# Rows of the heavy stage's first two batches prepared in the light stage, its zero columns on ScalarE

## The chip, the cores and the metric

One core of a Trainium2 chip runs the whole program in one launch. The metric is the device time of one execution in microseconds (us); of several runs the median is given. TensorE (PE in the rows) multiplies matrices, VectorE (DVE), ScalarE (ACT) and GpSimd (POOL) work on elements, and SyncE (SP) issues the transfers. Each engine takes its own instructions in program order and waits on semaphores for the others.

## What is computed

The program chains four layers on x of 16 x 512 tokens of 128 numbers: an attention with a distance kernel, a feed-forward layer, a state-space layer, and the same feed-forward layer again. The change lies in the feed-forward layer, which stands twice in the program (f1 and f2). Cut to what matters, it is:

```python
def _L0_ffn_ref(x, ...):
    light = local_attn(_ln(x, ln_w, ln_b), Wqkv, Wout_l)   # windowed attention, all tokens
    sq, iq = route(x, rt_q, NQ)                            # 64 tokens of each batch for queries
    skv, ikv = route(x, rt_kv, NKV)                        # 128 tokens of each batch for keys and values
    xq = x[br, iq]
    xkv = x[br, ikv]
    heavy = heavy_attn(xq, xkv, skv, gamma, Wq, Wkv, Wout_h, null_kv)   # begins with rms norm of xq, xkv
    out = jnp.broadcast_to(null_q[None, None, :], (b, n, d))
    out = out.at[br, iq].set(heavy)
    return out + light
```

## The kernel before

`stage_light` computes the local attention of all 16 batches and, beside it, the routing. Its loop has 64 steps, `step(t)`, four for each batch, and each step has two units. For a unit PE writes scores, VectorE takes maxima, ScalarE the exponentials, VectorE the reciprocals, GpSimd multiplies by them (`normalise`, L1481), PE turns the result and VectorE copies it out of PSUM (`f1l_pt`, L1192 to L1195), and PE multiplies by the values. Into these steps VectorE also puts the search for the routed tokens (`pick`), whose last pieces run in steps 60 and 61 (L1236, L1239, L1241, L1243). The projections of a batch (from `xh` and `xl`, the high and the low part of its normalised rows) run one batch ahead, so those of batch 15 are through before step 60, and `z`, `xh` and `xl` are not used again in this stage.

`stage_heavy` follows behind a barrier of all engines: each engine branches into the next block when all have left the last one. It treats the batches in eight pairs. For a pair, PE first gathers the routed tokens (`gather`, L1628 and L1629): for each batch `h` of the pair it multiplies the rows of the batch by a one-hot matrix `g`, eight matmuls of 128x256, alternating between the low part `yl` and the high part `yh` of the rows. `g` has 192 columns of one-hots, which VectorE writes for each batch (`onehots`, L1852 and L1855), and 64 columns of zeros behind them, written once for each of the two buffers at the start of the stage (L1905, VectorE). GpSimd makes `yh` and `yl` (`scaled`): it multiplies the layer's rows `y` by the rms factors `rc` into `yb` (L1814), copies this to `yh` (L1818), which rounds it, and subtracts to get `yl` (L1820). Two pairs of buffers, one for each batch of a pair, serve all batches in turn.

At the start of the stage PE first multiplies the null values by weights (`null_rows`, L1616), and then waits in `gather(0)` for `s_y` (GpSimd) and `s_g` (VectorE). When both gathers of a pair are done ScalarE takes the result out of PSUM (`tokens`, L1743, tile `gx`), and PE goes on with `queries` (L1638), `keys` (L1645), `contents` (L1653) and `scores` (L1668); nothing of a pair can start before `gx` is written. Then comes the gather of the next pair. GpSimd's program begins with `scaled(0)` and `scaled(1)`, then `scaled(2)` and `scaled(3)`, then `normalise(0, 0)` of the first pair.

Of the kernel before, what the change touches and what calls it, by code (L numbers as in the profile page):

```python
# [7 lines left out]
F32 = mybir.dt.float32  # L8
BF16 = mybir.dt.bfloat16
F32R = mybir.dt.float32r  # L10
ALU = mybir.AluOpType
# [3 lines left out]
P = 128  # L15
B, S, E = 16, 512, 128
NT = S // P
# [669 lines left out]
def stage_light(nc, K, tag, C=None):  # L687
# [13 lines left out]
    with ExitStack() as ctx:  # L701
# [3 lines left out]
        PW = P + W  # L705
        z = sb("z", [P, NT, P])
        xt = sb("xt", [P, S])
        xh = sb("xh", [P, 2, S], F32R)
        xl = sb("xl", [P, 2, S], F32R)
        qt = sb("qt", [P, 2, HP, S])  # L710
        kt = sb("kt", [P, 2, HP, S])
        vv = sb("vv", [P, 2, NT, 2, 2, 2, DH])
# [21 lines left out]
        s_xp = sem("xp")  # L734
        s_xe = sem("xe")
        s_xs = sem("xs")
        s_pp = sem("pp")
        s_pe = sem("pe")
        s_vs = [sem("vs0"), sem("vs1")]
# [719 lines left out]
        def _(pool):  # L1459
# [6 lines left out]
            def split(b):  # L1466
# [4 lines left out]
                pool.wait_ge(s_xs, 2 * b + 1)  # L1471
                nc.gpsimd.tensor_tensor(xl[:, par, :], xt[:], xh[:, par, :], ALU.subtract).then_inc(s_xs, 1)

            def normalise(n):
                u = n % UNITS
                pool.wait_ge(s_rs, n + 1)
                wait(pool, s_t, n - 1)
                r = rs[:, u % 2, :].unsqueeze(2)
                for cols, at in ((slice(0, P), 0), (slice(P, PW), HU * P)):
                    w = cols.stop - cols.start  # L1480
                    ins = nc.gpsimd.tensor_tensor(pn[:, u % 2, at:at + HU * w].rearrange("p (k c) -> p k c", k=HU),  # L1481
                                                  p[:, u % 2, :, cols], r.broadcast_to([P, HU, w]), ALU.mult)
                ins.then_inc(s_nm, 1)
# [19 lines left out]
            for t in range(T):  # L1503
                if t + 1 < T:
                    normalise(2 * t + 2)
                    normalise(2 * t + 3)
                if t % NT == TURN_AT and t // NT + 2 < B:
                    split(t // NT + 2)
                if t % NT == 1 and t // NT + 2 < B:
                    scaled(t // NT + 2)  # L1510

        work.close()
        sem.end()
# [2 lines left out]
def stage_heavy(nc, K, tag, stats, out=None):  # L1516
# [6 lines left out]
    with ExitStack() as ctx:  # L1523
# [4 lines left out]
        K1 = NKV + 1  # L1528
        GW = 256
        yb = sb("yb", [P, NT, P])  # L1530
        yh = sb("yh", [P, 2, NT, P], F32R)
        yl = sb("yl", [P, 2, NT, P], F32R)
        g = sb("g", [P, 2, NT, GW], F32R)
        gx = sb("gx", [P, 2, GC])
        rows = sb("rows", [P, M, S])
# [20 lines left out]
        s_yb = sem("yb")  # L1556
        s_nx = sem("nx")
        s_g = sem("g")
        p_w = sem("pw")
        v_w = sem("vw")  # L1560
        p_g = sem("pg")
# [50 lines left out]
        def _(pe):  # L1612
# [7 lines left out]
            def gather(m):  # L1620
                wait(pe, a_x, m)
                wait(pe, v_p, m - 1)
                for h in range(2):
                    pe.wait_ge(s_y, 2 * m + h + 1)
                    pe.wait_ge(s_g, 2 * m + h + 1)
                    at = W_[:, GB, h * GW:(h + 1) * GW]
                    for j in range(NT):
                        nc.tensor.matmul(at, yl[:, h, j, :], g[:, h, j, :], start=(j == 0), stop=False)  # L1628
                        mm = nc.tensor.matmul(at, yh[:, h, j, :], g[:, h, j, :], start=False, stop=(j == NT - 1))  # L1629
                    mm.then_inc(p_g, 1)  # L1630
# [108 lines left out]
        def _(act):  # L1739
# [43 lines left out]
            def values(m):  # L1783
# [2 lines left out]
                nc.scalar.activation(ot[:].rearrange("p c h q -> p h c q"),  # L1786
                                     W_[:, QB, :].rearrange("p (h c q) -> p h c q", h=2, c=HP), ACT.Copy).then_inc(a_ot, 1)

            for n in range(M + 1):
                if n >= 1:  # L1790
                    exps(n - 1, 0, (0, 1, 2, 3))
                    exps(n - 1, 1, (0, 1))
                if n < M:
                    tokens(n)
                if n >= 1:
                    exps(n - 1, 1, (2, 3))
                if n < M:
                    queries(n)
                    keys(n)
                if n >= 1:  # L1800
                    turned(n - 1)
                if n < M:
                    contents(n)
                if n >= 1:
                    values(n - 1)
# [4 lines left out]
        def _(pool):  # L1810
            def scaled(b):
# [1 line left out]
                t = slice(NT * b, NT * (b + 1))  # L1813
                nc.gpsimd.tensor_tensor(yb[:], K["y"][:, t, :], K["rc"][:, t].unsqueeze(2).broadcast_to([P, NT, P]),  # L1814
                                        ALU.mult).then_inc(s_yb, 1)
                pool.wait_ge(s_yb, 2 * b + 1)
                wait(pool, p_g, b - 1)
                nc.gpsimd.tensor_copy(yh[:, h], yb[:]).then_inc(s_yb, 1)  # L1818
                pool.wait_ge(s_yb, 2 * b + 2)
                nc.gpsimd.tensor_tensor(yl[:, h], yb[:], yh[:, h], ALU.subtract).then_inc(s_y, 1)  # L1820
                pool.wait_ge(s_y, b + 1)

            def normalise(m, h):
                pool.wait_ge(v_r, 2 * m + h + 1)
# [5 lines left out]
                nc.gpsimd.tensor_tensor(xp, xp, K["null_q"][:].unsqueeze(1).broadcast_to([P, 2 * NT, P]),  # L1830
                                        ALU.add).then_inc(s_nx, 1)

            scaled(0)
            scaled(1)
            for n in range(M + 1):
                if n >= 1:
                    normalise(n - 1, 0)
# [10 lines left out]
        def _(dve):  # L1848
# [52 lines left out]
                    ins = nc.vector.bn_aggr(K["mv"][:, 2 * NT * m + j, :], st6[:, j, :])  # L1901
                ins.then_inc(v_s, 1)

            for e in range(2):
                nc.vector.tensor_scalar(g[:, e, :, GC:], K["ident"][:, 0:GW - GC].unsqueeze(1)  # L1905
                                        .broadcast_to([P, NT, GW - GC]), 0.0, None, ALU.mult)
            onehots(0)
            onehots(1)
            dve.wait_ge(p_w, 1)
# [356 lines left out]
def program(nc, A, out):  # L2266
    with ExitStack() as ctx:
# [50 lines left out]
            C[n] = sb("c_" + n, [P, P])  # L2318
        for n in ("cc", "ss", "tmp", "dec"):
            C[n] = sb("c_" + n, [P, S])  # L2320
        with nc.sbuf_tensor("f1_y", [P, T, E], F32) as K["y"]:
            stage_light(nc, K, "f1", C)
            stage_heavy(nc, K, "f1", True)
        with nc.sbuf_tensor("f2_y", [P, T, E], F32) as K["y"]:
            stage_ssm(nc, K, C)
            stage_light(nc, K, "f2")
            stage_heavy(nc, K, "f2", False, out)
# [68 lines left out]
```

## Time and profile before

| | us |
|---|---|
| median of 3 runs | 1873.87 (1870.62 to 1874.62) |
| the profiled execution, its own time | 1877.24 |
| its span, from the first to the last instruction | 1875.2 |
| light stage f1, last instruction of VectorE ends | 1004.4 |
| heavy stage f1, first instruction of PE | 1004.72 |
| heavy stage f1, ScalarE begins to take out the first gather | 1013.99 |
| heavy stage f2, first instruction of PE | 1749.12 |

The rows below are read from the profiled execution. In a row of the order of time, the first number is the start of the instruction (or of a run of like instructions) in us from the start of the span, the second how long it took, then come the engine, the line, the operation, the tile written and those read, the shapes and the count; in brackets stands how long the engine had been idle before it, and what released it. "PEclk" in a table of stretches is the clock granted to TensorE as a share of 2.4 GHz; 0.50 is 1.2 GHz.

### The profile page before, as it was taken

Reading aid. Unit: us, or ns where it says so; the run is one execution under the profiler, and the core shown is the slowest. Engines: PE = TensorE matmul, PEld = TensorE weight load, DVE = VectorE, ACT = ScalarE, POOL = GpSimd, SP = SyncE. Lnnn points to the kernel's source line nnn. Section 1 sums busy time; section 2 is a strip of 40 time slices with the busy share of each in tenths; the row PEclk is TensorE's granted clock in tenths of the full one; section 3 lists DMA queues with packets and bytes.
Section 4 is the critical chain, followed back from the end, with each engine's and each line's share of the span. In section 5 each row is a group of like instructions: output and inputs, shape, how many; then the busy total and the mean of one; then the engine's idle time right before and its main releaser. Section 6 shows DMA issues by size and latency. Waiting matters only on the chain. (4 is left out here: it accounts for less than half of the span.)

```text
span 1875.2 us, 67956 instructions
## 1 busy us (share of the span) xinstructions
PE 1694.7 (90%) x27513; PEld 1302.1 (69%) x27513; DVE 1457.4 (78%) x3472; ACT 1434.4 (76%) x4088; POOL 752.5 (40%) x842
## 2 busy tenths in 40 slices
PE   3888888986999999999997996989999999998797
PEld 1444444444688888888885874668888888887586
DVE  8999999998577677877896766757777777789574
ACT  4999999995688888888773656668888888876364
POOL 2000000000254445454545866435454545454594
PEclk7999999998999999999998998989999999999898
DMA  6655655550000000101012000001010101010111
GB/s 194 153 142 143 160 136 144 125 149 4 12 20 19 20 20 15 24 14 25 14 25 47 2 2 1 1 12 23 16 25 15 25 14 26 14 25 15 45 46 46
DMA packets 80039, 91.94 MB, mean 49 GB/s; under 512 B 11696, under 2 KB 67984, under 8 KB 79728
## 3 DMA queue, kind: packets, MB, share of 16 engines
q1 hardware_dynamic: 78432, 87.15, 19.0%
q8 instruction: 220, 3.60, 0.8%
q14 instruction: 91, 0.75, 0.1%
q10 hardware_dynamic: 1296, 0.44, 0.1%
HBM read 39.68 MB, written 31.10 MB: 38 GB/s over the span
## 5 line engine op out<-in xcount | busy, mean ns | idle before, releaser
L1481 POOL TENSOR_TENSOR f1l_pn<-f1l_p,f1l_rs 128x512 f32<-128x512 f32 (+1 forms) x256 | 207.8, 833 | 264.6 <-DVE f1l_rs L1185 263.5
L1481 POOL TENSOR_TENSOR f2l_pn<-f2l_p,f2l_rs 128x512 f32<-128x512 f32 (+1 forms) x256 | 207.8, 833 | 256.0 <-DVE f2l_rs L1185 255.9
L1065 ACT ACTIVATE f2l_p<-f2l_sm,f2l_nb 128x192 f32<-128x192 f32 x512 | 214.6, 444 | 44.5 <-DVE f2l_nb L1178 44.5
L1065 ACT ACTIVATE f1l_p<-f1l_sm,f1l_nb 128x192 f32<-128x192 f32 x512 | 214.4, 443 | 42.4 <-DVE f1l_nb L1178 42.4
L412 PE MATMUL r_acc<-r_pr,r_vp 128*32 128x128 f32 (+2 forms) x3584 | 191.8, 330 | 7.1 <-DVE r_pr L625 6.0
L522 ACT ACTIVATE r_pr<-r_far 128x1536 f32<-128x1536 f32 x128 | 194.2, 1517 | 3.3 <-PE r_far L396 3.0
L617 DVE SCALAR_TENSOR_TENSOR r_pr<-r_pr,k_lo,r_cap 128x512 f32<-128x512 f32 x256 | 179.4, 741 | 6.5 <-ACT r_pr L522 6.3
L625 DVE TENSOR_SCALAR r_pr<-r_pr,k_hi,k_lo 128x768 f32<-128x768 f32 x256 | 164.3, 682 | 0.0
L522 ACT ACTIVATE r_pr<-r_near 128x1024 f32<-128x1024 f32 x128 | 138.5, 1082 | 1.1 <-PE r_near L383 1.1
L1486 POOL MEMSET k_rtz<- 128x608 f32 x1 | 0.6, 605 | 332.2 <-POOLq L683 332.2
L1178 DVE TENSOR_REDUCE f2l_nb<-f2l_sm 128x4 f32<-128x768 f32 x128 | 116.0, 947 | 8.2 <-PE f2l_sm L885 8.2
L1178 DVE TENSOR_REDUCE f1l_nb<-f1l_sm 128x4 f32<-128x768 f32 x128 | 115.9, 947 | 6.2 <-PE f1l_sm L885 6.2
L412 PEld LDWEIGHTS r_acc<-r_pr,r_vp 128*32 128x32 f32 x3584 | 87.2, 110 | 47.4 <-issue 29.0
L1065 ACT ACTIVATION_READ_ACCUMULATOR f2l_p<-f2l_sm,f2l_nb 128x1 f32 x512 | 117.2, 229 | 0.0
L1065 ACT ACTIVATION_READ_ACCUMULATOR f1l_p<-f1l_sm,f1l_nb 128x1 f32 x512 | 116.8, 228 | 0.0
L885 PE MATMUL f2l_sm<-f2l_kt,f2l_qt 64*64 64x128 f32 (+1 forms) x3584 | 99.4, 248 | 0.4 <-ACT f2l_p L1065 0.4
L885 PE MATMUL f1l_sm<-f1l_kt,f1l_qt 64*64 64x128 f32 (+1 forms) x3584 | 99.0, 248 | 0.0
L1203 DVE TENSOR_TENSOR f1l_ot<-f1l_xa,f1l_late 128x256 f32<-128x256 f32 x128 | 53.5, 418 | 57.6 <-ACT f1l_late L1057 57.0
L1203 DVE TENSOR_TENSOR f2l_ot<-f2l_xa,f2l_late 128x256 f32<-128x256 f32 x128 | 53.5, 418 | 57.4 <-ACT f2l_late L1057 56.8
L885 PEld LDWEIGHTS f2l_sm<-f2l_kt,f2l_qt 64*64 64x64 f32 x3584 | 92.9, 134 | 0.9 <-ACT f2l_p L1065 0.6
L925 PE MATMUL f2l_xa<-f2l_pt,f2l_vv 64*64 64x128 f32 x2048 | 85.8, 276 | 8.2 <-DVE f2l_pt L1193 3.4
L885 PEld LDWEIGHTS f1l_sm<-f1l_kt,f1l_qt 64*64 64x64 f32 x3584 | 92.8, 134 | 0.2 <-issue 0.2
(497 smaller groups left out, 5203.8 us busy)
## 6 DMA issues: line engine op xcount, KB each, us to landing
rbf_rows<-r_part SPq DMA_DIRECT2D x112, 128.0 KB, 2.3
r_qs<-rbf_rows SPq DMA_DIRECT2D x60, 192.0 KB
r_ks<-rbf_rows SPq DMA_DIRECT2D x60, 192.0 KB
f1l_vs<-f1l_vv SPq DMA_DIRECT2D x64, 128.0 KB, 2.4
f2l_vs<-f2l_vv SPq DMA_DIRECT2D x64, 128.0 KB, 2.4
rbf_rows<-r_part SPq DMA_DIRECT2D x16, 384.0 KB, 3.2
rbf_rows<-r_part SPq DMA_DIRECT2D x16, 256.0 KB, 3.2
out<-k_x SPq DMA_DIRECT2D x8, 512.0 KB, 3.2
```

Source lines behind the costliest of these rows:

```text
L412: mm = nc.tensor.matmul(acc[32 * g:32 * g + 32, q0:q0 + n], vp[:, par, t, g, 32 * q:32 * q + 32], pr[:, (PAIRS * b + 2 * q + g // 2) % RIN ...
L522: nc.scalar.activation(pr[:, n % RING, :, cols], src, ACT.Exp).then_inc(done, 1)
L617: nc.vector.scalar_tensor_tensor(on, on, K["lo"][:, h:h + 1], cap[:, h, :].unsqueeze(1).broadcast_to([P, NT, P]), ALU.max, ALU.min)
L625: ins = nc.vector.tensor_scalar(off, off, hi, lo, ALU.min, ALU.max)
L885: mm = nc.tensor.matmul(sm[64 * w:64 * w + 64, u % 2, e, cc * PW + P * side:cc * PW + P * side + kn], qt[r, par, c, at:at + W], kt[r, par, ...
L925: nc.tensor.matmul(xa[64 * e:64 * e + 64, r, cc * P:(cc + 1) * P], vv[rows, par, i, cc, g, e, :], pt[rows, u % 2, k * P:(k + 1) * P], star ...
L1065: ins = nc.scalar.activation(p[:, u % 2, k, :], sm[:, u % 2, k // 2, k % 2 * PW:(k % 2 + 1) * PW], ACT.Exp, bias=nb[:, u % 2, k:k + 1], ac ...
L1178: nc.vector.tensor_reduce(nb[:, u % 2, :], sm[:, u % 2, :, 0:2 * PW].rearrange("p a (k c) -> p a k c", k=2), AX, ALU.max, negate=True).the ...
L1203: nc.vector.tensor_tensor(ot[:, u // 2 % 2, 2 * g:2 * g + 2, :], xa[:, 0, 0:2 * P].rearrange("p (c q) -> p c q", q=P), late[:, u % 2, :].r ...
L1481: ins = nc.gpsimd.tensor_tensor(pn[:, u % 2, at:at + HU * w].rearrange("p (k c) -> p k c", k=HU), p[:, u % 2, :, cols], r.broadcast_to([P, ...
L1486: nc.gpsimd.memset(K["rtz"][:], 0.0).then_inc(s_rt, 1)
```

## The change

The buffers of the high and low rows, `xh` and `xl`, now outlive the light stage: they are allocated around both stages, the light stage uses them as before, and the heavy stage uses the same memory under its names `yh` and `yl`. At the end of steps 60 to 63 of the light stage GpSimd has a new function, `tokens(b, part)`, that does for batches 0 and 1 what `scaled(0)` and `scaled(1)` did in the heavy stage, with `z` in the place of `yb`: step 60 multiplies and copies batch 0, step 61 subtracts it, step 62 multiplies and copies batch 1, step 63 subtracts it. The heavy stage's GpSimd program begins with `scaled(2)`, and `gather(0)` waits no longer for rows. The zero columns of `g` are written by ScalarE as its first two instructions of the heavy stage, by a copy of `ident` with scale 0; `gather(0)` waits for them by a semaphore of its own (`a_g`).

```diff
@@ stage_light
-        xh = sb("xh", [P, 2, S], F32R)
-        xl = sb("xl", [P, 2, S], F32R)
+        xh, xl = K["xh"], K["xl"]
@@ stage_light, gpsimd
+            def tokens(b, part):
+                whole = z[:].rearrange("p j d -> p (j d)")
+                if part == 0:
+                    if b == 0:
+                        pool.wait_ge(s_xp, B)
+                        pool.wait_ge(s_pp, USES * B)
+                    t = bass.ds(b * NT, NT)
+                    nc.gpsimd.tensor_tensor(z[:], K["y"][:, t, :],
+                                            K["rc"][:, t].unsqueeze(2).broadcast_to([P, NT, P]), ALU.mult).then_inc(s_h, 1)
+                    pool.wait_ge(s_h, 3 * b + 1)
+                    nc.gpsimd.tensor_copy(xh[:, b, :], whole).then_inc(s_h, 1)
+                else:
+                    pool.wait_ge(s_h, 3 * b + 2)
+                    nc.gpsimd.tensor_tensor(xl[:, b, :], whole, xh[:, b, :], ALU.subtract).then_inc(s_h, 1)
+                    pool.wait_ge(s_h, 3 * b + 3)
...
                 if t % NT == 1 and t // NT + 2 < B:
                     scaled(t // NT + 2)
+                if t // NT == B - 1:
+                    tokens(t % NT // 2, t % NT % 2)
@@ stage_heavy
-        yh = sb("yh", [P, 2, NT, P], F32R)
-        yl = sb("yl", [P, 2, NT, P], F32R)
+        yh, yl = (K[n].rearrange("p h (j d) -> p h j d", j=NT) for n in ("xh", "xl"))
@@ stage_heavy, tensor, gather
-                    pe.wait_ge(s_y, 2 * m + h + 1)
+                    wait(pe, s_y, 2 * m + h - 1)
                     pe.wait_ge(s_g, 2 * m + h + 1)
+                    if m == 0:
+                        pe.wait_ge(a_g, h + 1)
@@ stage_heavy, scalar
+            for e in range(2):
+                nc.scalar.activation(g[:, e, :, GC:], K["ident"][:, 0:GW - GC].unsqueeze(1)
+                                     .broadcast_to([P, NT, GW - GC]), ACT.Copy, scale=0.0).then_inc(a_g, 1)
@@ stage_heavy, gpsimd (the waits on s_yb and s_y in scaled count from batch 2)
-            scaled(0)
-            scaled(1)
@@ stage_heavy, vector
-            for e in range(2):
-                nc.vector.tensor_scalar(g[:, e, :, GC:], K["ident"][:, 0:GW - GC].unsqueeze(1)
-                                        .broadcast_to([P, NT, GW - GC]), 0.0, None, ALU.mult)
```

The order of the instructions shows what has moved, here for f1; f2 reads alike. In the changed kernel the lines stand some 16 to 23 further down (L1497 is `normalise`, L1481 to L1487 are `tokens`, L1837 to L1843 are `scaled`). First GpSimd at the end of the light stage and the start of the heavy stage, before:

```order
L1481 TENSOR_TENSOR f1l_pn<-f1l_p,f1l_rs 128x256
L1512 UNCONDITIONAL_BRANCH
L1809 UNCONDITIONAL_BRANCH [waits barrier_Pool_Activation_PE_DVE_SP_gather]
L1814 TENSOR_TENSOR f1h_yb<-f_y,k_rc 128x512
L1818 CAST f1h_yh<-f1h_yb 128x512 [waits h_yb]
L1820 TENSOR_TENSOR f1h_yl<-f1h_yb,f1h_yh 128x512 [waits h_yb]
L1814 TENSOR_TENSOR f1h_yb<-f_y,k_rc 128x512 [waits h_y]
```

and now:

```order
L1497 TENSOR_TENSOR f1l_pn<-f1l_p,f1l_rs 128x256
L1481 TENSOR_TENSOR f1l_z<-f_y,k_rc 128x512
L1484 CAST f_xh<-f1l_z 128x512 [waits l_h]
L1487 TENSOR_TENSOR f_xl<-f1l_z,f_xh 128x512 [waits l_h]
L1530 UNCONDITIONAL_BRANCH [waits l_h]
L1832 UNCONDITIONAL_BRANCH [waits barrier_Pool_Activation_PE_DVE_SP_gather]
L1837 TENSOR_TENSOR f1h_yb<-f_y,k_rc 128x512
L1841 CAST f_xh<-f1h_yb 128x512 [waits h_pg,h_yb]
L1843 TENSOR_TENSOR f_xl<-f1h_yb,f_xh 128x512 [waits h_yb]
```

Batch 1 is now prepared behind the last normalisation of the light stage, ahead of the branch, and the first copy of the heavy stage is that of batch 2, which waits for PE's first gather (`h_pg`); batch 0 stands in the same way behind the normalisations of steps 60 and 61.

VectorE at the start of the heavy stage, before:

```order
L1209 TENSOR_TENSOR k_x<-k_x,f1l_xa 128x128 [waits l_w]
L1512 UNCONDITIONAL_BRANCH
L1847 UNCONDITIONAL_BRANCH [waits barrier_Pool_Activation_PE_DVE_SP_release]
L1905 TENSOR_SCALAR f1h_g<-k_ident 128x4x64 x2
L1852 TENSOR_TENSOR f1h_g<-k_iota,k_place 128x4x64
L1855 TENSOR_TENSOR f1h_g<-k_iota,k_place 128x4x128
```

and now:

```order
L1209 TENSOR_TENSOR k_x<-k_x,f1l_xa 128x128 [waits l_w]
L1530 UNCONDITIONAL_BRANCH
L1868 UNCONDITIONAL_BRANCH [waits barrier_Pool_Activation_PE_DVE_SP_release]
L1873 TENSOR_TENSOR f1h_g<-k_iota,k_place 128x4x64
L1876 TENSOR_TENSOR f1h_g<-k_iota,k_place 128x4x128
```

The one-hots of batch 0 are now the first instructions of VectorE in the stage; the two zero-column instructions stand on ScalarE ahead of the instruction that takes out the gather:

```order
L1170 ACTIVATE k_place<-f1l_pj 128x128 [waits l_tt]
L1530 UNCONDITIONAL_BRANCH
L1758 UNCONDITIONAL_BRANCH [waits barrier_Pool_Activation_PE_DVE_SP_release]
L1810 ACTIVATE f1h_g<-k_ident 128x4x64 x2
L1763 ACTIVATE f1h_gx<-f1h_ps,k_gam_h 128x384 [waits h_pg]
L1769 ACTIVATE f1h_qt<-f1h_ps 128x512 [waits h_pq]
```

These two instructions wait for nothing; before, the take-out (`f1h_gx`) was ScalarE's first instruction of the stage.

## Rows read from the trace of the kernel before

**Rows 1.** The page's busy time, share of the span and instructions of each engine.

```profile
PE 1694.7 (90%) x27513; PEld 1302.1 (69%) x27513; DVE 1457.4 (78%) x3472; ACT 1434.4 (76%) x4088; POOL 752.5 (40%) x842
```

**Rows 2.** Order of time, PE, start of the heavy stage f1, columns as told above.

```profile
1004.72 1.86 PE L1616 MATMUL f1h_ps<-k_wout_h,k_null_v 128*4 128x128 f32 x8 [0.65 <-PEq L1512]
1008.66 0.55 PE L1628 MATMUL f1h_ps<-f1h_g,f1h_yl 128*128 128x256 f32 x1 [2.07 <-DVE f1h_g L1855]
...
1010.29 0.41 PE L1629 MATMUL f1h_ps<-f1h_g,f1h_yh 128*128 128x256 f32 x1
1011.88 0.58 PE L1628 MATMUL f1h_ps<-f1h_g,f1h_yl 128*128 128x256 f32 x1 [1.18 <-POOL f1h_yl L1820]
...
1014.63 2.08 PE L1638 MATMUL f1h_ps<-f1h_gx,k_wq_h 128*128 128x128 f32 x8 [0.67 <-ACT f1h_gx L1743]
1016.50 3.02 PE L1645 MATMUL f1h_ps<-f1h_gx,k_wk_h 128*128 128x256 f32 x8
```

**Rows 3.** Order of time, PE, start of the heavy stage f2.

```profile
1749.12 1.86 PE L1616 MATMUL f2h_ps<-k_wout_h,k_null_v 128*4 128x128 f32 x8 [0.65 <-PEq L1512]
...
1756.28 0.58 PE L1628 MATMUL f2h_ps<-f2h_g,f2h_yl 128*128 128x256 f32 x1 [1.18 <-POOL f2h_yl L1820]
```

**Rows 4.** Order of time, DVE, start of the heavy stage f1.

```profile
1004.73 1.37 DVE L1905 TENSOR_SCALAR f1h_g<-k_ident 128x256 fp32r<-128x256 f32 x2 [0.33 <-PEq L1512]
1006.02 0.82 DVE L1852 TENSOR_TENSOR f1h_g<-k_iota,k_place 128x256 fp32r<-128x256 f32 x1
1006.77 1.75 DVE L1855 TENSOR_TENSOR f1h_g<-k_iota,k_place 128x512 fp32r<-128x512 f32 x1
```

**Rows 5.** Order of time, POOL, end of the light stage f1, start of the heavy stage.

```profile
990.93 3.33 POOL L1481 TENSOR_TENSOR f1l_pn<-f1l_p,f1l_rs 128x512 f32<-128x512 f32 x4 [3.27 <-DVE f1l_rs L1185]
1004.71 1.04 POOL L1814 TENSOR_TENSOR f1h_yb<-f_y,k_rc 128x512 f32<-128x512 f32 x1 [10.44 <-POOLq L1512]
1005.81 0.75 POOL L1818 CAST f1h_yh<-f1h_yb 128x512 fp32r<-128x512 f32 x1
1006.64 1.32 POOL L1820 TENSOR_TENSOR f1h_yl<-f1h_yb,f1h_yh 128x512 fp32r<-128x512 f32 x1
...
1010.24 1.59 POOL L1820 TENSOR_TENSOR f1h_yl<-f1h_yb,f1h_yh 128x512 fp32r<-128x512 f32 x1
```

**Rows 6.** Order of time, ACT, end of the light stage f1, start of the heavy stage.

```profile
1001.10 0.38 ACT L1057 ACTIVATE f1l_late<-f1l_xa 128x256 f32<-128x256 f32 x1 [1.36 <-PE f1l_xa L936]
...
1013.99 0.58 ACT L1743 ACTIVATE f1h_gx<-f1h_ps,k_gam_h 128x384 f32<-128x384 f32 x1 [12.28 <-PE f1h_ps L1629]
```

**Rows 7.** Stretches: length, busy us of PE, PEld, DVE, ACT, POOL; PEclk, DMA, GB/s.

```profile
1018.00:1019.00 1.00, 1.00 (x4) 0.79 (x4) 0.00 (x0) 0.55 (x1) 1.00 (x1) 0.62 0.00 0
1019.00:1020.00 1.00, 1.00 (x5) 0.68 (x4) 0.00 (x0) 0.50 (x2) 0.04 (x1) 1.00 0.00 0
```

**Rows 8.** Order of time, PE, the second pair's gather, queries and keys in f1.

```profile
1022.20 0.38 PE L1628 MATMUL f1h_ps<-f1h_g,f1h_yl 128*128 128x256 f32 x1
...
1024.09 0.28 PE L1629 MATMUL f1h_ps<-f1h_g,f1h_yh 128*128 128x256 f32 x1
1025.36 1.16 PE L1638 MATMUL f1h_ps<-f1h_gx,k_wq_h 128*128 128x128 f32 x8 [0.99 <-ACT f1h_gx L1743]
1026.36 1.89 PE L1645 MATMUL f1h_ps<-f1h_gx,k_wk_h 128*128 128x256 f32 x8
```

**Rows 9.** Order of time, POOL, steps 60 and 61 of the light stage f1.

```profile
976.10 3.92 POOL L1481 TENSOR_TENSOR f1l_pn<-f1l_p,f1l_rs 128x512 f32<-128x512 f32 x4 [3.33 <-DVE f1l_rs L1185]
983.22 2.06 POOL L1481 TENSOR_TENSOR f1l_pn<-f1l_p,f1l_rs 128x512 f32<-128x512 f32 x2 [3.20 <-DVE f1l_rs L1185]
```

**Rows 10.** Order of time, DVE, the same steps.

```profile
980.94 1.20 DVE L1239 TENSOR_TENSOR_SCAN f1l_some<-f1l_one,f1l_picks 32x512 f32<-32x512 f32 x1
```

**Rows 11.** Order of time, PE, the same steps.

```profile
985.28 0.67 PE L925 MATMUL f1l_xa<-f1l_pt,f1l_vv 64*64 64x128 f32 x16 [1.56 <-DVE f1l_pt L1193]
```

**Rows 12.** One line's instructions in f1: duration ns min/median/max, first and last start.

```profile
L1193 DVE COPY f1l_pt<-f1l_xa x128: 393/414/425, 503.0 to 998.0; 128x256 f32<-128x256 f32 x128
```

More of the change, by code:

```diff
@@ L736, in stage_light @@
         s_xs = sem("xs")
+        s_h = sem("h")
         s_pp = sem("pp")
@@ L1558, in stage_heavy @@
         s_g = sem("g")
+        a_g = sem("ag")
         p_w = sem("pw")
@@ L1815, in scaled @@
                                         ALU.mult).then_inc(s_yb, 1)
-                pool.wait_ge(s_yb, 2 * b + 1)
+                pool.wait_ge(s_yb, 2 * b - 3)
                 wait(pool, p_g, b - 1)
                 nc.gpsimd.tensor_copy(yh[:, h], yb[:]).then_inc(s_yb, 1)
-                pool.wait_ge(s_yb, 2 * b + 2)
+                pool.wait_ge(s_yb, 2 * b - 2)
                 nc.gpsimd.tensor_tensor(yl[:, h], yb[:], yh[:, h], ALU.subtract).then_inc(s_y, 1)
-                pool.wait_ge(s_y, b + 1)
+                pool.wait_ge(s_y, b - 1)
             def normalise(m, h):
@@ L2320, in program @@
             C[n] = sb("c_" + n, [P, S])
-        with nc.sbuf_tensor("f1_y", [P, T, E], F32) as K["y"]:
+        with (nc.sbuf_tensor("f1_y", [P, T, E], F32) as K["y"], nc.sbuf_tensor("f1_xh", [P, 2, S], F32R) as K["xh"],
+              nc.sbuf_tensor("f1_xl", [P, 2, S], F32R) as K["xl"]):
             stage_light(nc, K, "f1", C)
             stage_heavy(nc, K, "f1", True)
-        with nc.sbuf_tensor("f2_y", [P, T, E], F32) as K["y"]:
+        with (nc.sbuf_tensor("f2_y", [P, T, E], F32) as K["y"], nc.sbuf_tensor("f2_xh", [P, 2, S], F32R) as K["xh"],
+              nc.sbuf_tensor("f2_xl", [P, 2, S], F32R) as K["xl"]):
             stage_ssm(nc, K, C)
```

## The prediction

> **What bounds the kernel now.** I read the page's busy shares first, then the order of time on PE around both places where the light stage hands over to the heavy stage, then that of the other engines in the same microseconds, then the granted clock, and last the steps of the light stage into which the moved work is put.
>
> PE is busy for 90% of the span and GpSimd for 40% [rows 1], so a move of work off GpSimd matters only where PE waits for GpSimd. At the head of the heavy stage it does. PE ends `null_rows` at 1004.72 + 1.86 = 1006.58 and starts the first gather at 1008.66; the wait is put down to the one-hots [rows 2]. The second gather starts at 1011.88, after a wait for the low rows of batch 1, and ScalarE takes the result out at 1013.99 [rows 2, 6]. GpSimd ends the low rows of batch 0 at 1006.64 + 1.32 = 1007.96 and those of batch 1 at 1010.24 + 1.59 = 1011.83 [rows 5]. VectorE spends 1.37 on zero columns and ends the first one-hots at 1006.77 + 1.75 = 1008.52 [rows 4]. So the first gather waits for VectorE, with GpSimd 0.56 behind the same wait, and the second waits for GpSimd alone. Until the take-out nothing else of the pair can run: ScalarE had been idle for 12.28 [rows 6]. From the block's first matmul to the take-out are 13.99 - 4.72 = 9.27. In f2 the second gather also starts 7.16 after the first matmul, 1756.28 against 1749.12 [rows 3], so what f1 gains f2 gains too.
>
> All this runs at the low level of the clock. The stretch in which the granted clock goes up is 1018 to 1019 (0.62, then 1.00) [rows 7]: 1.2 GHz before it, 2.4 GHz behind it. What PE did before that was to work without a break from 1014.63; before, its work was cut by the two waits and by the take-out [rows 2].
>
> **The head of the heavy stage: 3.2 us each.** With the rows ready, the first gather waits for `null_rows` (1006.58), the zero columns and the first one-hots. The zero columns go to ScalarE: a row of 128x256 there took 0.38, one of 128x384 took 0.58 [rows 6]; two of them from 1004.72 on end between 1005.5 and 1005.9, under `null_rows`. If that cover were gone they would cost at most the 1.2 themselves. The one-hots: a VectorE instruction of this kind stands still while GpSimd works. The one at 1006.77 ran until 0.56 after GpSimd's subtraction ended (1008.52 against 1007.96) [rows 4, 5]; I take 0.56 as its own duration, and no more than that for the smaller one ahead of it. GpSimd still starts with a multiplication (1.04, until 1005.75 [rows 5]), then stands in its wait for the first gather. So the first one-hots end by 1005.75 + 0.56 + 0.56 = 1006.87, and 0.14 later, as at 1008.52 and 1008.66 [rows 2, 4], PE can start: 1007.0 at the latest of this reckoning, 1006.6 at the earliest (`null_rows`). I take 1006.9. The first gather lasts 1.85 (1008.66 to 1010.29, and 0.22 for the last of the eight), the second 2.11 up to the take-out (1011.88 to 1013.99) [rows 2, 6]; the second one-hots, 1.12 after the first, are in time. Take-out: 1006.9 + 1.85 + 2.11 = 1010.86 instead of 1013.99, a gain of 3.1 to 3.4; I take 3.2. The lower bound takes the one-hots as slow as they are now: 1008.52 - 1006.02 = 2.5 [rows 4] from 1004.73, so PE starts at 1007.37, and the second one-hots, 2.5 later still, hold up the second gather by 0.65 more; that leaves 2.0. VectorE's 1.37 of zero columns is part of this gain, not another term.
>
> What is late next is the hop through ScalarE (0.64 from 1013.99 to 1014.63 [rows 2, 6]) and PE's own work. GpSimd's copy of batch 2 now waits for the first gather at about 1008.8; behind it in its queue stand batches 2 and 3 and the normalisation of the first pair. With 0.75, 1.32, 1.04, 0.75 and 1.32 [rows 5] it is through by about 1014.5, and PE wants these rows behind the scores, at 1022.20 now [rows 8], some 3 to 6 earlier then. That is hidden by at least 1.5. SP's transfers stand in the same place as before.
>
> **The clock: 2.3 us each.** Without the two waits PE works from 1004.72 to 1010.4 with one gap of about 0.3. That is longer than its work from 1014.63 to the rise at 1018.6. So I expect the rise during the gathers, some 10 us earlier, and price it by rows at either level: queries 2.08 against 1.16, keys 3.02 against 1.89 [rows 2, 8], together 2.05; a gather 1.85 against 8 x (1024.09 - 1022.20) / 15 = 1.0 [rows 2, 8], so up to 0.85 more if the rise comes ahead of the second gather. From 2.0 to 2.9; I take 2.3. If the rise comes only behind the take-out, this term is near 0. The Trainium skill, TensorE: Matmul & The Clock Gate (Part 1: The HAM clock gate), says that the place of this rise shifts between runs of one kernel; no run here shows that yet.
>
> **The light stage: 0.2 us lost each.** `tokens` issues six GpSimd instructions per stage, 2 x (1.04 + 0.75 + 1.32) = 6.2 by [rows 5]. Batch 0's multiplication and copy fall behind the normalisations that end at 980.02, and the next normalisation starts at 983.22 after 3.20 of idle time [rows 9]; 1.79 fit, also with a wait in between. The subtraction (1.32) falls into the 3.27 ahead of 990.93, and batch 1 (3.1) into the 10.44 behind 994.26 [rows 5]. So no normalisation is late. What can be late is VectorE: its scan starts at 980.94 [rows 10], while GpSimd's multiplication would run until about 981.1, and reads SBUF alone as the one-hots do. PE waits for VectorE just behind it (1.56 at 985.28 [rows 11]), so this wait is on the path: 0.2. Bounds: 0, if the scan doesn't mind, and 1.0, if it also waits for the copy (981.1 + 0.1 + 0.75). Nothing is taken out of the light stage, so it can't gain. VectorE's copies out of PSUM don't mind GpSimd: L1193 took 393 to 425 ns in all 128 cases [rows 12], many of them beside a normalisation.
>
> The Trainium skill, SBUF — State Buffer (SBUF: two separate sides), says that VectorE and GpSimd share a port pair as an exclusive lock for a whole instruction, taken on VectorE's side by operations with two SBUF inputs. By that rule the scan loses the 0.2, and without it 0; the end at 1008.52, 0.56 behind GpSimd's, agrees with it.
>
> **Sum.** 3.2 + 2.3 - 0.2 = 5.3 per stage, 10.6 for both. The profiled execution's own 1877.24 would become 1866.6. It lies 3.4 above the median of the runs shown, 1873.87; taken from the median, the forecast is 1863.3.
>
> **The rivals.**
> - *The clock rises early in one stage only, or in neither.* For it: the take-out still cuts PE's work, and before, two pieces of some 2 us each and a third of 1.9 behind a gap of 0.67 had not raised it by 1018 [rows 2, 7]. Against it: the first stretch is now 5.7 long. One stage only: 1863.3 + 2.3 = 1865.6; neither: 1867.9.
> - *Another wait takes the place of GpSimd's*, so that the change doesn't do what it says: one-hots as slow as now (a gain of 2.0), the scan at its worst (1.0), no earlier clock. 2 x 1.0 gained, 1871.9, within 0.2%. For it: VectorE was the last releaser of the first gather [rows 2]. Against it: its slowness came from GpSimd's work beside it, of which 1.04 is left.
> - *GpSimd's moved work stops VectorE in the light stage.* The mechanism is the lock between the two, in steps 60 to 63: if VectorE stood still for the whole of `tokens`, the light stage would lose 6.2 per stage against 3.2 gained, without the earlier clock. 1873.87 + 2 x 3.0 = 1879.9. It decides from a loss of 3.2 per stage on. For it: PE waits for VectorE there [rows 11]. Against it: VectorE's work there is mostly out of PSUM, in which GpSimd's work doesn't show [rows 12], and half of the 6.2 falls where VectorE itself waits for the last outputs.
>
> **How the numbers follow.** Forecast, early clock in both stages: 0.40. In one: 0.23; in neither: 0.21; another wait: 0.10; the light stage loses more: 0.06. The range takes in the first three with their bounds: at the low end 3.4 + 2.9 - 0 = 6.3 per stage, 1861.3, and a little less for the spread of the runs (3.3 below the median): 1860.0; at the high end no early clock, 2.0 - 0.2 = 1.8 per stage, 1870.3, so 1870.5. A measurement of this kernel can tell about 0.2%, 3.7 us, from no change. Faster by more: 0.40 + 0.23 + 0.21 = 0.84; within: 0.10; slower: 0.06.
>
> **What would show it.** In the changed kernel's order of time: the first gather within 0.5 of the end of `null_rows`, the second right behind it, and the take-out 5.5 to 6.2 after the block's first matmul, where it is 9.27 now. The clock at 1.00 before the queries, which then take about 1.2, not 2.1. The scan's end at most 0.3 later against the normalisation ahead of it, and the last 28 us of the light stage (976.10 to 1004.4) as long as before within 0.5. Wrong would be: a first gather that still waits for VectorE beyond 1.0, queries at 2.08, or VectorE instructions in steps 60 to 63 that take longer than now beside `tokens`.

## The result, and the profile after

The changed kernel takes 1857.79 us (median of 4 runs, 1855.63 to 1863.65) against 1872.71 of the kernel before beside it: a ratio of 0.992, 95% interval 0.9902 to 0.9939. It is faster, as forecast, but by 14.9 us (by the interval 11.4 to 18.4) instead of 10.6, and the time lies 2.2 below the low end of the range. The profiled execution took 1859.21, its span 1857.4 (before: 1877.24 and 1875.2). Two of all the executions here, one of the kernel before (2116.78) and one of the changed kernel (1952.04), were in a slower state of the chip and are left out of every median below.

Order of time, PE, end of the light stage f1 and head of the heavy stage, changed kernel (it answers to [rows 2]):

```profile
1003.74 1.16 PE L947 MATMUL f1l_xa<-k_wout_l,f1l_ot 128*128 128x128 f32 x8 [0.60 <-DVE f1l_ot L1203]
1005.55 1.03 PE L1634 MATMUL f1h_ps<-k_wout_h,k_null_v 128*4 128x128 f32 x8 [0.65 <-PEq L1530]
1007.51 0.39 PE L1648 MATMUL f1h_ps<-f1h_g,f_xl 128*128 128x256 f32 x1 [0.93 <-DVE f1h_g L1876]
...
1009.41 0.28 PE L1649 MATMUL f1h_ps<-f1h_g,f_xh 128*128 128x256 f32 x1
1010.36 1.16 PE L1658 MATMUL f1h_ps<-f1h_gx,k_wq_h 128*128 128x128 f32 x8 [0.67 <-ACT f1h_gx L1763]
...
1014.90 1.11 PE L1688 MATMUL f1h_ps<-f1h_kt,f1h_qt 64*64 64x129 f32 x32
```

The wait for GpSimd's low rows (1.18 in [rows 2]) is gone: the sixteen matmuls of both gathers run in a row from 1007.51. The queries start 4.8 behind the block's first matmul, where it was 9.9, and take 1.16 instead of 2.08. `null_rows` takes 1.03 instead of 1.86, and the light stage's last output ahead of it 1.16: here PE comes into the heavy stage at 2.4 GHz already. In f2 of the same execution it does not:

```profile
1736.08 2.08 PE L947 MATMUL f2l_xa<-k_wout_l,f2l_ot 128*128 128x128 f32 x8 [0.60 <-DVE f2l_ot L1203]
1738.80 1.86 PE L1634 MATMUL f2h_ps<-k_wout_h,k_null_v 128*4 128x128 f32 x8 [0.65 <-PEq L1530]
1740.76 0.58 PE L1648 MATMUL f2h_ps<-f2h_g,f_xl 128*128 128x256 f32 x1
...
1742.00 0.40 PE L1649 MATMUL f2h_ps<-f2h_g,f_xh 128*128 128x256 f32 x1
1742.21 0.31 PE L1648 MATMUL f2h_ps<-f2h_g,f_xl 128*128 128x256 f32 x1
...
1744.26 0.94 PE L1658 MATMUL f2h_ps<-f2h_gx,k_wq_h 128*128 128x128 f32 x6 [0.67 <-ACT f2h_gx L1763]
```

Here the first gather starts without a wait, and its matmuls change from 0.40 to 0.28 towards its end. The stretches of the changed kernel show the clock (columns as in [rows 7]; the granted clock stands behind POOL's busy time):

```profile
1006.00:1008.00 2.00, 1.07 (x10) 0.74 (x8) 2.00 (x4) 0.25 (x1) 0.58 (x1) 1.00 0.39 137
...
1740.00:1742.00 2.00, 1.90 (x10) 1.37 (x8) 2.00 (x7) 0.00 (x0) 0.00 (x0) 0.50 0.80 232
1742.00:1744.00 2.00, 1.59 (x12) 1.38 (x11) 1.45 (x4) 0.38 (x1) 1.14 (x2) 0.94 1.04 227
```

So in f1 it is 1.00 from the start, and in f2 it rises at about 1742.2, 3.4 behind the block's first matmul, where it was some 14 ([rows 7], within 1018 to 1019, against 1004.72).

VectorE and ScalarE at the head of f1, order of time, changed kernel ([rows 4, 6]):

```profile
1005.55 1.30 DVE L1873 TENSOR_TENSOR f1h_g<-k_iota,k_place 128x256 fp32r<-128x256 f32 x1 [0.32 <-PEq L1530]
1006.78 0.68 DVE L1876 TENSOR_TENSOR f1h_g<-k_iota,k_place 128x512 fp32r<-128x512 f32 x1
```

```profile
1005.53 0.72 ACT L1810 ACTIVATE f1h_g<-k_ident 128x256 fp32r<-128x256 f32 x2 [2.08 <-PEq L1530]
1009.73 0.58 ACT L1763 ACTIVATE f1h_gx<-f1h_ps,k_gam_h 128x384 f32<-128x384 f32 x1 [3.48 <-PE f1h_ps L1649]
```

ScalarE's zero columns are through at 1006.25, in `null_rows`' shadow. The take-out comes 4.18 behind the block's first matmul (9.27 before).

GpSimd in the last steps of the light stage f1 and at the head, and VectorE's scan, order of time, changed kernel ([rows 5, 9, 10]):

```profile
981.73 1.04 POOL L1481 TENSOR_TENSOR f1l_z<-f_y,k_rc 128x512 f32<-128x512 f32 x1
982.83 1.47 POOL L1484 CAST f_xh<-f1l_z 128x512 fp32r<-128x512 f32 x1
984.96 2.06 POOL L1497 TENSOR_TENSOR f1l_pn<-f1l_p,f1l_rs 128x512 f32<-128x512 f32 x2 [0.67 <-DVE f1l_rs L1185]
...
997.08 0.61 POOL L1484 CAST f_xh<-f1l_z 128x512 fp32r<-128x512 f32 x1
...
1005.54 1.04 POOL L1837 TENSOR_TENSOR f1h_yb<-f_y,k_rc 128x512 f32<-128x512 f32 x1 [6.50 <-POOLq L1530]
```

```profile
982.68 1.20 DVE L1239 TENSOR_TENSOR_SCAN f1l_some<-f1l_one,f1l_picks 32x512 f32<-32x512 f32 x1
```

The scan takes 1.20 as before. It is GpSimd's copy that waits, 1.47 where the second one takes 0.61, and the normalisation behind it still has 0.67 to spare.

**Where the 17.8 between the two spans went**, by the starts of the same instructions on PE. The first scores of f1 before, in the order of time:

```profile
1021.16 1.11 PE L1668 MATMUL f1h_ps<-f1h_kt,f1h_qt 64*64 64x129 f32 x32
```

From the heavy stage's first matmul in f1 to the first of the state-space stage: 122.4 before, 114.4 after, a gain of 8.0, of which 7.1 lie ahead of the first scores (16.44 against 9.35 behind the block's first matmul). In f2, from the same matmul to the end: 126.1 and 118.6, a gain of 7.5, of which 6.3 ahead of the first scores (16.29 against 9.99). The state-space stage, from its first matmul to the end of its last: 101.1 and 99.6, a gain of 1.5. The rest, 0.8, lies in all that comes ahead and in the light stage of f2; what comes ahead alone differs by up to 7 between executions of one kernel (the heavy stage of f1 starts between 1003.67 and 1010.60 in four profiles of the changed kernel). The profile of before is of an execution 4.5 above the median beside the result, that of the changed kernel of one 1.4 above its own, which is why 17.8 here is 14.9 in the medians.

### The profile page after: what moved, and what is told of

Its sections match the earlier page's. It is cut to its first block and busy times, and to the rows that moved or that the text cites. A ratio compares the mean times of both kernels' runs of the same rounds, so it can differ in the third digit from the quotient of the medians.

```text
span 1857.4 us, 67964 instructions
## 1 busy us (share of the span) xinstructions
PE 1684.3 (91%) x27513; PEld 1292.5 (70%) x27513; DVE 1448.5 (78%) x3468; ACT 1436.0 (77%) x4092; POOL 753.7 (41%) x842
## 5 line engine op out<-in xcount | busy, mean ns | idle before, releaser
L1497 POOL TENSOR_TENSOR f1l_pn<-f1l_p,f1l_rs 128x512 f32<-128x512 f32 (+1 forms) x256 | 207.9, 834 | 259.6 <-DVE f1l_rs L1185 258.6
L1497 POOL TENSOR_TENSOR f2l_pn<-f2l_p,f2l_rs 128x512 f32<-128x512 f32 (+1 forms) x256 | 207.9, 834 | 250.7 <-DVE f2l_rs L1185 250.7
```

## The experiments

The theory: both head waits fell, and the clock with them, so the gain lies ahead of the first scores; the light stage loses little. The rivals: the zero columns did it; the moved GpSimd work has a price in the light stage; or the clock alone did it. All of the first group ran beside each other and one set of runs of before (1873.26).

**The changed kernel again.**

> The changed kernel as it is, run again on another occasion, for its time over more runs and a second profile. Theory A (the rows' waits at both heads of the heavy stage are gone and TensorE's clock is up early there; what exceeds this differs from run to run with the places at which the clock happens to fall): the heads give 6.3 to 7.1 us each, so 13 to 15 us below the kernel before, and from block start to the first scores 9.3 to 10.0 us in both stages where the kernel before took 16.3 to 16.4; whether the light stage's last output runs at 1.2 or 2.4 GHz may come out either way in each stage. Theory B (the light stage itself became shorter by the change, 27.4 us instead of 28.3 us for its last part in f1): the last output runs at 2.4 GHz again in f1.

1857.11, ratio 0.9922 (0.9906 to 0.9939). Its heads were the other way round: f1 came in at 1.2 GHz (first scores after 10.1) and f2 at 2.4 (9.3). Over four profiles of the changed kernel five of eight heads came in at 2.4 GHz (9.33 to 9.35) and three at 1.2 (9.99 to 10.09); the mean is 9.6. So which one does is not fixed by the program. A head that comes in at 2.4 GHz also ends its light stage 0.9 sooner (22.87 against 23.78 from VectorE's scan to the heavy stage, f1 and f2 of the first profile). Over the kernels here that put no dummy matmuls into the light stage, nine of fourteen heads behind a light stage with the moved work came in at 2.4 GHz, and one of six behind one without it; whether the moved work makes this likelier is not shown by so few.

**The rows moved, the zero columns left on VectorE.**

```diff
@@ changed kernel, stage_heavy: a_g and its waits out
-            for e in range(2):
-                nc.scalar.activation(g[:, e, :, GC:], ... ACT.Copy, scale=0.0).then_inc(a_g, 1)
@@ vector
+            for e in range(2):
+                nc.vector.tensor_scalar(g[:, e, :, GC:], ... 0.0, None, ALU.mult)
             onehots(0)
```

> Only the rows are moved; the zero columns stay on VectorE ahead of the one-hots. Theory A: VectorE's first instruction stands still for GpSimd's 1.04 us, the first one-hots come 0.6 to 0.7 us later than in the changed kernel, at about 2.5 us after the block's start, and the time is 0.5 to 2.5 us above the changed kernel's, so 11 to 14 us below the kernel before. Theory C (the zero columns on VectorE were the larger part of the wait): 4 us or more above the changed kernel's.

1860.09, ratio 0.9932 (0.9919 to 0.9945). PE and VectorE at its head, order of time:

```profile
1002.20 1.03 PE L1633 MATMUL f1h_ps<-k_wout_h,k_null_v 128*4 128x128 f32 x8 [0.65 <-PEq L1530]
1004.56 0.39 PE L1645 MATMUL f1h_ps<-f1h_g,f_xl 128*128 128x256 f32 x1 [1.33 <-DVE f1h_g L1870]
```

```profile
1002.20 1.37 DVE L1920 TENSOR_SCALAR f1h_g<-k_ident 128x256 fp32r<-128x256 f32 x2 [0.33 <-PEq L1530]
1003.50 0.41 DVE L1867 TENSOR_TENSOR f1h_g<-k_iota,k_place 128x256 fp32r<-128x256 f32 x1
1003.83 0.68 DVE L1870 TENSOR_TENSOR f1h_g<-k_iota,k_place 128x512 fp32r<-128x512 f32 x1
```

The two zero-column instructions of f1 apart (duration ns min/median/max, first and last start):

```profile
L1920 DVE TENSOR_SCALAR f1h_g<-k_ident x2: 280/726/1172, 1002.2 to 1003.3; 128x256 fp32r<-128x256 f32 x2
```

The first gather starts 2.36 behind the block's first matmul, 0.4 later than in the changed kernel. The first zero-column instruction takes 1.17 beside GpSimd's multiplication (1002.18 to 1003.22), the second, behind it, 0.28, and the one-hots 0.41 and 0.68. In the changed kernel the first one-hots take 1.30 instead, because now they meet that multiplication. What VectorE loses at the head is thus the multiplication, whichever of its instructions stands first: most of what ScalarE takes off VectorE is lost again, and the rows carry nearly the whole gain. Both heads came in at 2.4 GHz, with the first scores after 9.73 and 9.74.

**The zero columns on ScalarE, the rows left.** The same instructions the other way, in the kernel before.

> Only the zero columns go to ScalarE; the rows are prepared in the heavy stage as before. Theory A: the second gather still waits for the low rows of batch 1, about 7.1 us after the block's start, so the time is that of the kernel before within 1.5 us. Theory C: 4 us or more below the kernel before.

1875.30, ratio 1.0013 (1.0003 to 1.0024): nothing gained. The first gather started 3.5 instead of 3.9 behind the block's first matmul, the second where it was, since it waits for GpSimd, and the first scores came at 16.3 and 16.4. Of the two parts it is the zero columns that are worth nothing alone.

**The light stage's work twice.** `tokens` as in the changed kernel, added to the kernel before; its result is not used.

> The kernel before, with the six GpSimd instructions of the preparation added to the light stage's last four steps (their result is not used; the heavy stage prepares its rows as before). It prices what the moved work costs the light stage. Theory A: nothing, the time of the kernel before within 1.5 us, and the scan still takes 1.20 us. The prediction's step: 0.2 us per stage, at most 1.0 per stage. Theory B: the light stage gets shorter by it, 1.8 us or more in all below the kernel before.

1873.64, ratio 0.9996 (0.9982 to 1.001). No cost of the moved work in the light stage can be told: the interval is from 3.4 us faster to 1.9 slower, and from VectorE's scan (1.20) to the heavy stage it is 22.85 in f1 and 23.77 in f2, where two light stages without that work have 22.86 and 23.78 at the same clock. f1 of the profiled execution came into the heavy stage at 2.4 GHz, with the old waits. Order of time, PE, and the stretches:

```profile
1006.84 1.03 PE L1635 MATMUL f1h_ps<-k_wout_h,k_null_v 128*4 128x128 f32 x8 [0.65 <-PEq L1531]
1010.78 0.55 PE L1647 MATMUL f1h_ps<-f1h_g,f1h_yl 128*128 128x256 f32 x1 [2.90 <-DVE f1h_g L1874]
...
1014.00 0.58 PE L1647 MATMUL f1h_ps<-f1h_g,f1h_yl 128*128 128x256 f32 x1 [1.17 <-POOL f1h_yl L1839]
...
1016.74 2.08 PE L1657 MATMUL f1h_ps<-f1h_gx,k_wq_h 128*128 128x128 f32 x8 [0.67 <-ACT f1h_gx L1762]
```

```profile
1010.00:1011.00 1.00, 0.22 (x1) 0.25 (x2) 1.00 (x2) 0.00 (x0) 0.92 (x2) 0.77 1.05 217
1011.00:1012.00 1.00, 1.00 (x6) 1.00 (x7) 1.00 (x2) 0.00 (x0) 0.94 (x2) 0.50 1.05 207
...
1020.00:1021.00 1.00, 1.00 (x5) 0.80 (x4) 0.00 (x0) 0.44 (x1) 1.00 (x1) 0.61 0.00 0
```

The clock was up at 1006.84, fell in the wait of 2.90, and rose again only in 1020 to 1021. The first scores came after 16.4, as in the kernel before. So with the waits left empty this head, which came in at 2.4 GHz, lost the clock; in the changed kernel's five it stayed up to the queries.

**The clock without the rows.** A second group, beside 1873.6 of before. In the kernel before, dummy matmuls stand in PE's two waits, so that the clock rises while the gathers still wait; their result is not used.

```diff
@@ kernel before, stage_heavy, tensor
+            def busy(k):
+                for c in range(k):
+                    nc.tensor.matmul(W_[:, TB, 0:P], K["wq_h"][:, 0:P], K["wq_h"][:, 0:P], start=True, stop=True)
...
                 for h in range(2):
+                    if m == 0:
+                        busy((4, 2)[h])
                     pe.wait_ge(s_y, 2 * m + h + 1)
```

> The kernel before with nothing moved, but PE kept at work in the two waits at the head of the heavy stage: four 128x128 fp32 matmuls, not used, behind null_rows and two between the gathers. It prices the clock by itself, with the waits for the rows left in. Theory A (clock and waits both count): the clock is up 4 to 7 us after the block's start, queries take about 1.2 us instead of 2.1 us, and the first scores start at 12.7 to 13.5 us after the block's start instead of 16.2 to 16.5: 6 to 7 us below the kernel before. Theory D (only the waits count, the clock comes back where it did): the time of the kernel before within 1.5 us.

1868.17, ratio 0.9974 (0.9964 to 0.9984), 5.4 us, a little less than expected. Order of time, PE, f1:

```profile
1008.28 1.86 PE L1616 MATMUL f1h_ps<-k_wout_h,k_null_v 128*4 128x128 f32 x8 [0.65 <-PEq L1512]
1010.08 1.90 PE L1622 MATMUL f1h_ps<-k_wq_h 128*128 128x128 f32 x8
1012.23 0.36 PE L1634 MATMUL f1h_ps<-f1h_g,f1h_yl 128*128 128x256 f32 x1 [0.25 <-DVE f1h_g L1861]
...
1015.45 0.39 PE L1634 MATMUL f1h_ps<-f1h_g,f1h_yl 128*128 128x256 f32 x1 [1.59 <-POOL f1h_yl L1826]
...
1017.34 1.16 PE L1644 MATMUL f1h_ps<-f1h_gx,k_wq_h 128*128 128x128 f32 x8 [0.67 <-ACT f1h_gx L1749]
...
1021.88 1.11 PE L1674 MATMUL f1h_ps<-f1h_kt,f1h_qt 64*64 64x129 f32 x32
```

Both gathers still start where they did, the second 7.17 behind the block's first matmul as in [rows 2], and the first scores come at 13.6 instead of 16.4, in f2 as well: this is the clock alone, 2.8 per stage. The changed kernel with the same `null_rows` (1.86) has them at 10.0 to 10.1: the waits are worth 3.6 more. The clock alone is thus less than half of the gain, and that rival falls.

**GpSimd's first multiplication later.** It waits until VectorE has written both one-hots.

```diff
@@ changed kernel, stage_heavy, gpsimd, scaled
+                if b == 2:
+                    pool.wait_ge(s_g, 2)
                 nc.gpsimd.tensor_tensor(yb[:], K["y"][:, t, :], ...
```

> The changed kernel, with GpSimd's first multiplication of the heavy stage made to wait for the one-hots of batches 0 and 1, so that VectorE has its first instructions for itself. Theory A (what is left of the first gather's wait is VectorE standing still for GpSimd's 1.04 us): the first one-hots need 0.41 + 0.68 us, the first gather starts at 1.1 to 1.3 us after the block's start where the clock is up at the block's start (1.9 now) and at 1.9 to 2.0 where it isn't (null_rows ends then), 0.2 to 1.7 us below the changed kernel in all. Rival: GpSimd becomes late with batches 2 and 3, and the second pair's gather waits for it: at or above the changed kernel.

1857.41, ratio 0.9916 (0.9900 to 0.9932), beside 1858.26 of the changed kernel (third time, below): not told apart. VectorE and PE at the head of f2, order of time:

```profile
1739.43 0.42 DVE L1875 TENSOR_TENSOR f2h_g<-k_iota,k_place 128x256 fp32r<-128x256 f32 x1 [0.33 <-PEq L1530]
```

```profile
1739.43 1.03 PE L1634 MATMUL f2h_ps<-k_wout_h,k_null_v 128*4 128x128 f32 x8 [0.65 <-PEq L1530]
1740.51 0.38 PE L1648 MATMUL f2h_ps<-f2h_g,f_xl 128*128 128x256 f32 x1
```

The one-hots take 0.42 where they took 1.30, and the wait of 0.93 ahead of the first gather is gone: it starts 1.1 behind the block's first matmul instead of 1.9, and the first scores come at 8.5. In a head that comes in at 1.2 GHz `null_rows` (1.86) covers nearly the whole of it (9.8, against 10.0 without).

**The clock kept up into the heavy stage.** As the last, with twelve dummy matmuls in PE's last waits of the light stage (two and three in each of steps 62 and 63, two ahead of the last output; the first expectation below counts eleven).

```diff
@@ stage_light, tensor
+            def busy(k):
+                for c in range(k):
+                    nc.tensor.matmul(sm[:, 0, 0, 0:P], K["ident"][:], K["ident"][:], start=True, stop=True)
...
+                if t + 2 >= T:
+                    pe.wait_ge(s_ex, UNITS * B - 1)
+                    busy(2)
```

> As e5_mult_later, and PE is kept at work in its waits of the light stage's last two steps by seven... eleven unused 128x128 fp32 matmuls in all (two ahead of the first and three ahead of the second values of steps 62 and 63, two ahead of the last output), so that the clock stays up into the heavy stage. Theory A: the last output takes 1.1 to 1.2 us and null_rows 1.03 us in both stages, the first scores start 8.4 to 8.7 us after the block's start in both, 2 to 4 us below the changed kernel in all. Rival: the added matmuls stand in the way of the values and the outputs, and the light stage's last part gets longer by as much or more: at or above the changed kernel.

1857.40 (0.9914, 0.9897 to 0.9931), and a second time, in a third group (before: 1871.79) and beside 1857.36 of the changed kernel, 1857.99 (0.9929, 0.9909 to 0.9948):

> The changed kernel with the two additions of the last call: GpSimd's first multiplication of the heavy stage waits for the one-hots of batch 1, and twelve dummy matmuls of 128x128 stand in TensorE's last waits of the light stage. Theory that the clock at the head is the whole rest of the gain: both heads have block start to scores 8.4 instead of 9.3 to 10.1, so 2 to 3 us below the changed kernel beside it. Rival, that the dummies stand in the way of real work at the light stage's end or that the runs of the changed kernel have the high clock there about as often: equal to the changed kernel within 1.5 us.

All four heads came in at 2.4 GHz, with the first scores at 8.45 to 8.46, 1.1 less than the changed kernel's mean. In the time nothing can be told from the changed kernel, and the 2 to 4 us expected did not show; 2.3 us for both heads was to be seen at best, and the clock fell elsewhere: in the second profile it stood low for 3.4 from 984 on, in the last steps of f1's light stage, and the stretch from the scan to the end of that stage was 1.4 longer (24.26 against 22.87). f2 of the run with the later multiplication, without dummy matmuls, has such a stretch too (24.38).

**The changed kernel a third and a fourth time**, as the neighbours of these:

> The changed kernel beside the three above on the same chip, for a direct comparison and a third profile: 1855 to 1860 us; block start to first scores 9.3 us where the clock is up at the block's start and 10.0 us where it isn't.

> The changed kernel again, as the neighbour of the next two runs. All theories: 1857 to 1859 us, ratio to before 0.992.

1858.26 and 1857.36, ratios 0.9923 (0.9910 to 0.9936) and 0.9929 (0.9908 to 0.9949).

**The same at the head of the state-space stage.** As the kernel with the light stage's twelve dummy matmuls, and nine more behind that stage's first transpose, where PE waits for the input.

```diff
@@ stage_ssm, tensor
+            for k in range(9):
+                nc.tensor.matmul(tp[:, 0, 0:P], K["ident"][:], K["ident"][:], start=True, stop=True)
```

> As the run before it, with nine more dummy matmuls of 128x128 on TensorE at the start of the state-space stage, behind its first transpose, where TensorE waits for the input transfer. Theory that the clock at a stage's head is worth its rows at either level wherever a stage begins: the first products of that stage (3.7 us at the low level in the changed kernel, 1.9 at the high one) end some 1.8 earlier, so 1 to 2 us below the run before it, 1854 to 1856. Rival, that VectorE's scan and not TensorE sets the time there: equal to the run before it within 1 us.

1855.48, ratio 0.9918 (0.9901 to 0.9935). Order of time, PE, the changed kernel first, then this one:

```profile
1119.94 0.45 PE L2211 MATMUL s_xx<-k_ident,k_c_bb 128*128 128x128 f32 x1 [3.94 <-PEq L1955]
...
1128.11 3.49 PE L2230 MATMUL s_xx<-s_ut,s_bbt 128*64 128x512 f32 x8 [1.30 <-ACT s_ut L2150]
...
1133.82 1.94 PE L2230 MATMUL s_xx<-s_ut,s_bbt 128*64 128x512 f32 x8 [1.21 <-ACT s_ut L2150]
```

```profile
1119.34 0.45 PE L2223 MATMUL s_xx<-k_ident,k_c_bb 128*128 128x128 f32 x1 [3.94 <-PEq L1967]
1119.58 3.38 PE L2225 MATMUL s_tp<-k_ident 128*128 128x128 f32 x18
...
1126.87 1.94 PE L2244 MATMUL s_xx<-s_ut,s_bbt 128*64 128x512 f32 x8 [1.54 <-ACT s_ut L2162]
...
1131.03 1.94 PE L2244 MATMUL s_xx<-s_ut,s_bbt 128*64 128x512 f32 x8 [1.20 <-ACT s_ut L2162]
```

The second block of products starts 11.7 instead of 13.9 behind the transpose: 2.2 gained at that place. The median is 1.9 to 2.5 below its two neighbours, and the lowest of all kernels here, but the runs of the three overlap (1854.79 to 1858.32 against 1854.35 to 1859.93 with the light stage's dummies alone and 1854.37 to 1862.23 of the changed kernel), so that it beats the changed kernel is likely and not shown.

## Why the prediction was too small

The mechanism was right and sizes were off: the clock's term was priced for one level of the clock only, and the state-space stage, in which 1.5 came, was put at nothing without a reason.

**Right.** What bounds the head (two waits, then the take-out), that both stages gain, the sign, and that the clock adds to it. The queries take 1.16 in all eight heads.

**Wrong: the sizes in the sum, 5.3 per stage.** The gain ahead of the first scores is 16.4 - 9.6 = 6.8 on average:

- *The head, forecast 3.2:* 3.6, from 13.6 with the clock alone to 10.0 with the rows ready. The sum took both gathers at their length at the low clock, which puts the second 4.0 behind the block's first matmul. The clock rises during the first gather: in f2 the second starts after 3.7 (sixteen matmuls in a row from 1740.76), and the take-out comes after 4.2 to 4.9 instead of the forecast 5.5 to 6.2. The gain by the waits and the gain by the clock are not two independent terms, and no run has the rows ready and the clock low throughout, so the waits by themselves are not measured.
- *The clock, forecast 2.3, at most 2.9:* 2.8 if PE comes in at 1.2 GHz, and 0.7 more (10.0 against 9.3) if it comes in at 2.4, which five of eight heads did; 3.2 on average. This is the step of the sum that failed: the bound of 2.9 was too low. It allowed for a rise ahead of the second gather at the earliest, and did not ask what a head without waits does with a clock that is already up: it keeps it. The rows of before had shown both heads at 1.2 GHz (`null_rows` 1.86, [rows 2, 3]) and I took that for fixed.
- *The light stage, forecast -0.2:* 0 as far as can be told. VectorE's scan was expected to stand behind GpSimd's multiplication. It started 0.09 before that ended and took 1.20; GpSimd's copy waited for it instead, in 0.67 and more of idle time. The Trainium skill, SBUF — State Buffer (SBUF: two separate sides), says that the one that starts first has the shared ports for its whole instruction. By that rule the loss depends on who is first, and the trace agrees in the main: the copy took 1.47 behind the scan's start, the one-hots 1.30 beside GpSimd's multiplication and 0.42 without it; but the copy ended only 0.42 behind the scan, less than the 0.61 it takes alone, and the scan, begun in the last 0.09 of the multiplication, took no longer for it.

Two readings of the rows were wrong as well. The 1.37 of zero columns is mostly a stop beside GpSimd's multiplication, 1.17 and 0.28 in one stage; it passes to whichever VectorE instruction comes first, so moving them is worth 0.4 per head at the scores (9.73 against 9.35). And the larger one-hots take 0.68 alone, not 0.56.

Both stages together: 2 x 6.8 = 13.6 against the 10.6 of the sum.

**Not in the sum at all: 1.5 in the state-space stage.** That stage lasts 100.9 to 101.1 in the profiles of before and of the experiments with only part of the change or with dummy matmuls in the kernel before, and 99.6 to 99.7 in all four of the changed kernel. Order of time, PE, and a stretch of before; then PE of the changed kernel:

```profile
1164.48 2.86 PE L2223 MATMUL s_yy<-k_c_g,s_v 64*128 64x128 f32 x32
1167.28 2.84 PE L2228 MATMUL s_yy<-k_c_dd,s_ut 128*128 128x128 f32 x16
```

```profile
1166.00:1168.00 2.00, 2.00 (x17) 1.78 (x14) 0.69 (x2) 2.00 (x6) 1.36 (x2) 0.50 0.00 0
```

```profile
1157.45 2.06 PE L2241 MATMUL s_yy<-k_c_g,s_v 64*128 64x128 f32 x32
1159.44 2.05 PE L2246 MATMUL s_yy<-k_c_dd,s_ut 128*128 128x128 f32 x16
```

Before, the clock falls once more there and these take 2.86 and 2.84; in the changed kernel it does not. The waits around it are the same in both (2.03 and 2.47 or 2.48 ahead of `s_ty`). What makes the fall come or stay out is not settled; no run here varied it alone. 13.6 + 1.5 = 15.1, near the 14.9 measured. The run with the rows alone fits: its heads gain 2 x 6.6, its state-space stage next to nothing, and it came out 13.2 below the kernel before.

**The range.** Its low end stood on 6.3 per stage, 12.6 (1861.3, less 1.3 for the spread). The heads gave 1.0 more than that, the state-space stage 1.5, and the kernel before was 1.2 lower beside the result (1872.71) than where the forecast set out (1873.87). With the heads alone and from 1873.87 the time would have been 1860.3, just inside: that it fell outside is in part chance.

The rivals: that the clock rises early in one stage or in none fell, since it was up ahead of the queries in all eight heads of the changed kernel. Another wait did take a place, VectorE's first one-hots (0.93 at 1007.51), as feared; it is too short to matter, and where PE comes in at 1.2 GHz it is covered. That the moved work stops VectorE in the light stage was taken out by the run with the work done twice. Of what was to be seen, the first gather came 0.1 behind the end of `null_rows` in f2 but 0.93 in f1, not within 0.5, and the end of the light stage was 0.9 shorter where PE came in at 2.4 GHz; the rest held or was better.

## What to carry to other kernels

A wait at the head of a stage costs itself and the clock of what follows: count both, and count the clock from the stage's first matmul, at both levels, since PE may come in at either. When a bound rests on a clock level seen in one profile, work out the sum for the other level too, and put the end of the range there. And of a term that shifts work beside another engine, ask which of the two starts first: here the one that came second paid.

## What was not expected of the hardware

- The level of the clock at the same place differs between executions of one kernel: the light stage's last output took 1.16 in five and 2.08 in three of eight stage ends of the changed kernel. The Trainium skill, TensorE: Matmul & The Clock Gate (Part 1: The HAM clock gate), says that the place of the rise shifts between runs; these profiles show a fall that comes in some executions and not in others.
- In the run with the light stage's work twice the clock fell in a wait of 2.90, 3.7 behind the block's first matmul, and was low for 10. In the changed kernel's heads that came in low it rose after 3.4 to 3.7.
- VectorE stood still beside GpSimd's multiplication with one input too: the first zero-column instruction took 1.17, the second 0.28.
- A GpSimd copy of 128x512 took 0.61 alone and 1.47 beside VectorE's scan, and up to 2.37 at the head in the run with the later multiplication.
